# An adaLN block on one core: batch 1's normalised rows turned by VectorE and DMA, and a set of small edits to loads and scaling

## The reference

```python
mod = (_silu(c) @ wmod).reshape(4, 6, 1, 512)
sa, ca, ga, sb, cb, gb = (mod[:, i] for i in range(6))
ga = (2 * (ga >= 0) - 1) * jnp.maximum(jnp.abs(ga), 0.25)      # gb likewise
h = _layernorm(x) * (1 + ca) + sa
q, k, v = split(h @ Wqkv + bqkv)                                 # 128 columns each
attn = softmax(q @ k.T / sqrt(128)) @ v
x = x + ga * (attn @ Wo + bo)
h = _layernorm(x) * (1 + cb) + sb
top1 = argmax(h @ gate_w.T + expert_bias)                        # of 4 experts
x = x + gb * (h @ W_up.T + lora_B[top1] @ (lora_A[top1] @ h))
```

## Time and profile before

| | us |
|---|---|
| three timed runs | 182.58, 185.03, 185.26 (median 185.03) |
| profiled execution, whole | 182.96 |
| its span | 181.2 |
| TensorE busy in the span | 170.8 (94%) |
| VectorE busy | 139.6 (77%) |
| ScalarE, GpSimd busy | 90.1, 80.4 |

### The profile page before, as it was taken

One profiled execution on the slowest core, in us unless ns is written; L12 is line 12 of the kernel. 1 busy time (PEld: TensorE's weight loads), 2 busy tenths in 40 slices (PEclk: granted clock), 3 DMA queues, 4 the chain that ended last, 5 costly groups with the idle time before them and its releaser, 6 DMA issues.

```text
span 181.2 us, 2841 instructions
## 1 busy us (share of the span) xinstructions
PE 170.8 (94%) x924; PEld 134.9 (74%) x924; DVE 139.6 (77%) x352; ACT 90.1 (50%) x170; POOL 80.4 (44%) x109
## 2 busy tenths in 40 slices
PE   6867999999999999999999999999999999999990
...
GB/s 130 313 352 379 387 385 234 269 206 52 0 54 183 0 0 50 98 109 157 0 114 33 213 139 83 0 0 56 65 149 26 0 2 0 0 4 58 174 41 190
DMA packets 13918, 21.32 MB, mean 118 GB/s; under 512 B 3356, under 2 KB 4128, under 8 KB 13904
## 3 DMA queue, kind: packets, MB, share of 16 engines
...
## 4 chain that ended last, share of the span: by engine, by line
PE 57%; DVE 18%; ACT 8%; SPq 6%; DMA 6%; issue 4%; POOL 0%; DVEq 0%; ACTq 0%; POOLq 0%
PE bank L400 37%; SPq L322 5%; DMA stage<-in_L_wmod_dram 4%; PE bank L414 3%; DVE xs L1236 3%; ACT xn_p L849 3%; DVE stats L1243 3%; DVE xn L1169 2%; PE bank L524 2%; DVE f_gb L1301 1%; DVE h1lo L1158 1%; DVE h2lo L1174 1%; PE bank L509 1%; PE bank L503 1%; DMA stage<-xn 1%
## 5 line engine op out<-in xcount | busy, mean ns | idle before, releaser
L400 PE MATMUL bank<-wup_lo,h2hi 128*128 128x512 f32 (+1 forms) x68 | 27.2, 401 | 0.4 <-ACT h2hi L907 0.4
L400 PE MATMUL bank<-wup_hi,h2hi 128*128 128x512 f32 (+1 forms) x68 | 26.0, 382 | 0.0
L888 ACT ACTIVATE xn_p<-xs,shift,rstd 128x512 f32<-128x512 f32 x16 | 13.1, 816 | 25.9 <-POOL shift L1498 25.8
L400 PE MATMUL bank<-wup_hi,h2lo 128*128 128x512 f32 (+1 forms) x68 | 25.9, 381 | 0.0
L1495 POOL TENSOR_TENSOR rstd<-var_eps,neg_half 128x1 f32<-128x1 f32 x16 | 8.9, 554 | 37.2 <-DVE var_eps L1247 37.2
L1510 POOL TENSOR_TENSOR xs<-xs,f_gb 128x512 f32<-128x512 f32 x14 | 17.9, 1292 | 7.7 <-DVE f_gb L1301 7.7
L400 PE MATMUL bank<-h1lo,wqkv_hi 128*128 128x512 f32 x48 | 19.7, 411 | 1.6 <-ACT wqkv_hi L881 1.2
L1487 POOL TENSOR_TENSOR xs<-xs,gabo 128x512 f32<-128x512 f32 x16 | 20.3, 1308 | 0.1
L400 PE MATMUL bank<-h1hi,wqkv_hi 128*128 128x512 f32 x48 | 19.0, 395 | 0.0
L400 PE MATMUL bank<-h1hi,wqkv_lo 128*128 128x512 f32 x48 | 18.9, 394 | 0.0
L1219 DVE TENSOR_TENSOR plo<-bank,phi 128x512 fp32r<-128x512 f32 x16 | 10.0, 684 | 6.7 <-ACT phi L857 6.6
...
## 6 DMA issues: line engine op xcount, KB each, us to landing
...
stage<-in_L_wmod_dram SPq DMA_DIRECT2D x3, 1024.0 KB, 8.0
xs<-in_L_wmod_dram SPq DMA_DIRECT2D x3, 1024.0 KB, 7.6
xs<-in_L_attn_x_dram SPq DMA_DIRECT2D x3, 1024.0 KB, 8.4
...
f_gb<-in_L_ffn_W_up_dram SPq DMA_DIRECT2D x1, 1024.0 KB, 11.4
...
```

Source lines behind the costliest of these rows:

```text
L400: mm = nc.tensor.matmul(dst, w, m, start=first and i == 0, stop=last and i == total - 1)
L888: nc.scalar.activation(xn2_p[:, t, :], xs[:, b, t, :], ACT.Identity, bias=shift[:, 1, t:t + 1], scale=rstd[:, 1, t:t + 1]).then_inc(S["xn2 ...
```

## The change

- `TURNED` is 1: batch 1 too goes by blocks. Its 16 transposes on TensorE are gone; VectorE turns its four tiles around `qk_low(0)`, SyncE issues the 16 moves straight behind the load of gb, and x of batch 2 is loaded behind them. The first statistics of batch 2 stand behind batch 1's `h1_low`.
- Around that the order of the work changes: w_up's transposes come ahead of `pv(0)`, `modulation(3)` ahead of `out_projection(0)`, all of batch 1's qkv behind it.
- Loads: x of batch 0 in two halves, no waits between the first loads; sb and cb go to `f_gb`, w_up to `xs[:, 2]`; wo and bo ahead of w_up.
- ca is loaded and multiplied in two halves of 256 columns, each with its own bank.
- The scale of the scores is multiplied into Wq and q's bias by GpSimd (`scale_wq`), so `maxima` is one instruction per tile.
- eps of the second layer norm is added by GpSimd and not by VectorE.
- ga is spread over the partitions by transposes (line 445 before) and not by products.
- `gate_ffn(b - 1, 0)` stands ahead of the first tile's statistics.

The diff, cut to its core:

```diff
 
-TURNED = 2
...
+        (5, "cT"), (0, "x1T", 0, 0), (1, "x1T", 0, 1), (2, "x1T", 0, 2), (3, "x1T", 0, 3), (6, "mod", 0), (5, "ca_half"),
...
         (7, "PT", 0, 0), (1, "PT", 0, 1), (3, "PT", 0, 2), (0, "PT", 0, 3),
-        (2, "x1T", 1, 0), (4, "x1T", 1, 1), (6, "x1T", 1, 2), (7, "x1T", 1, 3), (5, "O", 0),
...
-        raw = {"ca": stage[:], "sa": xs[:, 2], "ga": xs[:, 3], "sb": stage[:], "cb": stage[:], "gb": xs[:, 3],
-               "wup": f_gb, "wqkv": xn2_p}
+        raw = {"ca": stage[:], "sa": xs[:, 2], "ga": xs[:, 3], "sb": f_gb[:], "cb": f_gb[:], "gb": xs[:, 3],
+               "wup": xs[:, 2], "wqkv": xn2_p}
...
             sp.dma_start(c_rows[0:B, :], c).then_inc(c_in, 16)
-            for i, ts in enumerate((slice(0, 1), slice(1, 2), slice(2, 4))):
-                sp.dma_start(xs[:, 0, ts], x_v[0, :, ts, :]).then_inc(x0_in[i], 16)
-            load_section("ca")
-            sp.wait_ge(x0_in[1], 16)
+            for i in range(2):
+                sp.dma_start(xs[:, 0, 2 * i:2 * i + 2], x_v[0, :, 2 * i:2 * i + 2, :]).then_inc(x0_in[i], 16)
+            for half in range(2):
+                sp.dma_start(raw["ca"][:, :, columns_of(half)], wmod_v[SECTION["ca"], :, :, columns_of(half)]).then_inc(ca_in[half], 16)
             load_wqkv((0, 1))
-            sp.wait_ge(x0_in[2], 16)
             load_section("sa")
             load_wqkv((2, 3))
             sp.wait_ge(S["bqkv_zero"], 1)
             sp.dma_start(bqkv_rows[0:B, :], bqkv.partition_broadcast(B)).then_inc(bqkv_in, 16)
             sp.dma_start(xs[:, 1], x_v[1]).then_inc(x_in[1], 16)
             load_section("ga")
-            wait_used(0)
             load_section("sb")
-            wait_used(1)
-            sp.dma_start(xs[:, 2], x_v[2]).then_inc(x_in[2], 16)
             sp.dma_start(wo_raw[:], wo).then_inc(wo_in, 16)
             sp.dma_start(bo_bc[:], bo.partition_broadcast(P)).then_inc(bo_in, 16)
-            sp.dma_start(raw["wup"][:], wup.rearrange("(o p) h -> p o h", p=P)).then_inc(wup_in, 16)
+            wait_used(1)
+            sp.dma_start(raw["wup"], wup.rearrange("(o p) h -> p o h", p=P)).then_inc(wup_in, 16)
             sp.dma_start(ga_rows[0:E, :], gate_w).then_inc(ga_rows_in, 16)
             sp.dma_start(ga_rows[E:GZ, :], lora_a.rearrange("e r h -> (e r) h")).then_inc(ga_rows_in, 16)
             for e in range(E):
...
             wait_used(2)
             load_section("cb")
             load_section("gb")
+            move_turned(1)
+            sp.wait_ge(S["wupT_psum"], NK)
+            sp.dma_start(xs[:, 2], x_v[2]).then_inc(x_in[2], 16)
             write_gate(0)
             spread_gate(0, 1)
             wait_used(3)
...
                     pe.wait_ge(mod_in[s], 16)
-                if g == 0:
-                    pe.wait_ge(S["silu_step"], 4)
                 quarters = [(s, kt) for s in GROUPS[g] for kt in range(0, NK, len(GROUPS[g]))]
                 for more in range(len(GROUPS[g])):
                     for i, (s, kt) in enumerate(quarters):
                         mm = nc.tensor.matmul(dst[i * QUARTER:(i + 1) * QUARTER, :], silu_wide[:, kt + more, :],
                                               raw[s][:, kt + more, :], start=more == 0, stop=more == len(GROUPS[g]) - 1)
                 mm.then_inc(S["mod_psum"], 1)
+
+            def first_modulation():
+
+                pe.wait_ge(S["silu_step"], 4)
+                for half in range(2):
+                    dst = open_bank("ca_half") if half else open_bank("mod", 0)
+                    pe.wait_ge(ca_in[half], 16)
+                    for kt in range(NK):
+                        mm = nc.tensor.matmul(dst[kt * QUARTER:(kt + 1) * QUARTER, columns_of(half)], silu_wide[:, kt, :],
+                                              raw["ca"][:, kt, columns_of(half)], start=True, stop=True)
+                    mm.then_inc(S["mod_psum"] if half else S["ca_half_psum"], 1)
 
             def first_modulation_columns(half):
...
@@ -719,16 +719,14 @@
             first_gate_everywhere()
             gate_to_rows("ga")
             p_transposes(0, (3,))
-            x1_transposes(1)
+            w_up_transposes(range(NK))
             pv(0)
-            w_up_transposes(range(NK))
-            qkv(1, (0,))
+            modulation(3)
             out_projection(0)
-            qkv(1, (1,))
-            modulation(3)
+            qkv(1, (0, 1))
             gate_transposes()
+            qkv(1, (2,))
             lora_b_transposes()
-            qkv(1, (2,))
             modulation_columns(3)
             qkv(1, (3,))
             x2_transposes(0)
...
                     nc.scalar.activation(xn2_p[:, t, :], at("S", b, t)[:], ACT.Exp, bias=neg_max[:, t:t + 1],
-                                         scale=SCORE_SCALE, accum_out=row_sum[:, t:t + 1]).then_inc(S["p_ready"], 1)
+                                         accum_out=row_sum[:, t:t + 1]).then_inc(S["p_ready"], 1)
...
@@ -878,6 +876,7 @@
 
             def wqkv_high(kt):
                 act.wait_ge(wqkv_in[kt], 16)
+                act.wait_ge(S["wq_scaled"], kt + 1)
...
             act.wait_ge(S["ga_bc_psum"], 1)
             nc.scalar.activation(ga_bc[:, 0, :], at("ga_bc")[:], ACT.Copy).then_inc(S["ga_bc_ready"], 1)
             pt_high(0, (3,))
-            h1_high(1, (0, 1))
+            wup_high((0, 1))
             wo_high(0)
-            h1_high(1, (2, 3))
+            wup_high((2, 3))
             o_high(0)
-            wup_high(range(NK))
+            h1_high(1)
+            modulation_rows(3)
             ln2_normalise(0, (0, 1))
-            modulation_rows(3)
...
                 dve.wait_ge(S["x1T_psum"], NK)
                 for t in range(NT):
-                    nc.vector.tensor_scalar(xn1[:, t, :], xs[:, 1, t, :], moments[:, 0, t, 0:1], rstd[:, 0, t:t + 1],
+                    nc.vector.tensor_scalar(xn1_blocks[:, :, :, t].rearrange("p a k i -> p k a i"),
+                                            xs[:, 1, t, :].rearrange("p (k a i) -> p k a i", k=NK, a=NB),
+                                            moments[:, 0, t, 0:1], rstd[:, 0, t:t + 1],
                                             ALU.subtract, ALU.mult).then_inc(S["xn1_ready"], 1)
...
-            def turn_blocks(b):
-                for t in range(NT):
+            def turn_blocks(b, tiles=range(NT)):
+                for t in tiles:
                     xn1_done(dve, b, t + 1)
                     nc.vector.transpose(xn1_blocks[:, :, :, t], xn1_blocks[:, :, :, t]).then_inc(S["xn1_turned"], 1)
...
             def maxima(b):
                 for t in range(NT):
                     dve.wait_ge(S["S_psum"], NT * b + t + 1)
-                    nc.vector.reduce_max(row_max[:, t:t + 1], at("S", b, t)[:], AX_X).then_inc(S["max_ready"], 1)
-                    dve.wait_ge(S["max_ready"], NT * b + t + 1)
-                    nc.vector.tensor_scalar(neg_max[:, t:t + 1], row_max[:, t:t + 1], -SCORE_SCALE, None,
-                                            ALU.mult).then_inc(S["negmax_ready"], 1)
+                    nc.vector.reduce_max(neg_max[:, t:t + 1], at("S", b, t)[:], AX_X, negate=True).then_inc(S["negmax_ready"], 1)
...
@@ -1243,9 +1241,6 @@
                 nc.vector.bn_stats(stats[:, 1, t, :], xs[:, b, t, :]).then_inc(S["ln2_stats"], 1)
                 dve.wait_ge(S["ln2_stats"], NT * b + t + 1)
                 nc.vector.bn_aggr(moments[:, 1, t, :], stats[:, 1, t, :]).then_inc(S["ln2_aggr"], 1)
-                dve.wait_ge(S["ln2_aggr"], NT * b + t + 1)
-                nc.vector.tensor_scalar(var_eps[:, 1, t:t + 1], moments[:, 1, t, 1:2], LN_EPS, None,
-                                        ALU.add).then_inc(S["ln2_var"], 1)
...
@@ -1343,9 +1338,11 @@
             widen_sa()
             second_ln1_normalise()
             qkv_shift_row()
+            turn_blocks(1, (0,))
             qkv_shift()
+            turn_blocks(1, (1, 2))
             qk_low(0)
-            ln1_stats(2, (0, 1))
+            turn_blocks(1, (3,))
             maxima(0)
             add_parts("ga")
             gate_columns("ga")
@@ -1353,17 +1350,19 @@
             v_low(0)
             pt_low(0)
             gate_rows_evacuate("ga")
-            h1_low(1)
+            wup_low(range(NK))
             split_sb()
             inverse_sums(0)
             o_low(0)
-            wup_low(range(NK))
+            h1_low(1)
+            ln1_stats(2, (0,))
             for t in range(NT):
                 residual(0, t)
...
+            ln1_stats(2, (1,))
...
                     for t in range(NT):
                         residual(b, t)
+                        if t == 0:
+                            gate_ffn(b - 1, 0)
                         ln2_moments(b, t)
-                        if t != 1:
-                            gate_ffn(b - 1, (0, 0, 1, 2)[t])
+                        if t >= 2:
+                            gate_ffn(b - 1, t - 1)
                     gate_ffn(b - 1, 3)
...
             def ln2_deviation(b, tiles):
```

(21 more changed lines are left out.)

43 lines of the change are left out of this document (18 added, 25 removed).

## The result

The changed kernel takes 185.22 us (median of 20 runs, 184.29 to 187.2), the kernel before 182.63 us beside it (181.89 to 186.07): a ratio of 1.016, interval 1.014 to 1.018. (The ratios of this text leave out executions in a slower state that the chip shows with either kernel, so this one differs a little from the ratio of the medians.) The change is slower by 1.6%, where I had forecast 181.7 us and a gain of 2.3; the time lies above my range, which ended at 184.8. The profiled execution took 185.26 us, its span is 183.5 (before 182.96 and 181.2).

The account below looks back on a forecast made before the run. TensorE bounds most of the span, but VectorE's new chain decides: 1.0 + 0.2 + 0.8 = 2.0 us by batch 2's scores, plus 0.3 at the end, gain 2.3. Middle of 180.7 and 182.8: 181.7 us, range 178.9 to 184.8.

Parts of the forecast that it names:

- TensorE's work: TensorE's queue: batch 1's 16 transposes go (1.75 us) and ga's products become transposes (0.56 us), together 2.3 us less.
- the scaling of Wq: On GpSimd between 11 and 17 us, four pieces: costed at nothing, under 1 us were the cover gone.
- A = 41.9: Landing of batch 1's last move: first move at 30.5 us, last begins 9.4 later and lands 2.02 after that.
- break-even of 42.9: VectorE ahead of batch 1's scores: landing time at which it breaks even; the forecast landing left it 1.0 us early.
- A + 3.6: VectorE after the last landing of batch 1's moves: its next own work after the four h1_lo begins 3.6 us later.
- The residual cycles (1.6 us): VectorE ahead of batch 1's scores: four residuals with their statistics, 1.6 us each instead of 1.81, 6.4 in all.
- From the second tile on a gain: Second normalisation, eps by GpSimd: 0.3 us each, a loss of 0.1 for a single tile, then a gain.
- 0.8 us of gain from four shorter residuals: Batch 2's chain up to its scores: four residuals 0.2 us shorter each, 0.8 of the 2.0 us gained there.
- The end: Last batch: earlier statistics close most of h2hi's 0.4 us wait, counted 0.3; f_gb's 0.4 wait goes too, not added.
- as I thought likeliest: Whole kernel: time within 2% (3.7 us) of before, the first and third cases, 0.68 less 0.03.
- My third: VectorE's chain eats the gain: landing at 44 by slower moves or late gb, gain 0.2, 182.8 us; chance 0.18.
- The fourth: SyncE can't issue the moves while cb and gb are on their way: landing at 49.4, 188.2 us; chance 0.10.

Follow-up runs that it names:

- e_no_turn: The changed kernel with batch 1's rows transposed by TensorE again, all other parts kept; 1.001 (0.998-1.004) against the kernel before.

## Why the turning costs: two engines at one port

Two of the turning's terms could be undone by order alone, so I tried these, the sum of them, and one of them without the turning.

```diff
 # f_quiet, against the changed kernel
-            add_output_bias(0)
+            add_output_bias(0, (0, 1))
+            pool.wait_ge(S["h1_lo"], NK * 2)
+            add_output_bias(0, (2, 3))
 # f_early_ga: batch 2's ga rows behind batch 1's, no longer behind the moves
             spread_gate(0, 1)
+            spread_gate(0, 2)
...
-                if b + 2 < B:
+                if b and b + 2 < B:
                     spread_gate(0, b + 2)
 # f_all: both, and eps on VectorE; f_best: e_no_turn with early rows and eps on VectorE
```

> The changed kernel; GpSimd adds the output bias to the first two tiles of batch 0 as it did, and waits with the last two until h1_lo of batch 1 is through. Theory (the first two h1_lo of batch 1 take 1361 and 1790 ns in place of 746 because GpSimd adds the bias to tiles 2 and 3 meanwhile, both engines reading two operands from SBUF): all four h1_lo take 0.75 us or less, VectorE's first residual starts 1.3 to 1.7 us earlier, tiles 2 and 3 of the bias (1.3 us each) are still in time for residuals 2 and 3, and the time falls by 1.0 to 1.6 us against the change: 0.7 to 1.1% above the kernel before. Rival (the long h1_lo come from the load of x2, which lands in xs at the same time): they stay at 1.4 to 1.8 us, the time stays at +1.6% or grows, since GpSimd is later.

> The changed kernel with batch 2's ga rows spread straight behind batch 1's, instead of behind the 16 moves of batch 2 and the two spreads of gb. Theory (at batch 1's second normalisation GpSimd is the chain, since ga's rows land only at 87.7 us and 2.6 us of output weights and bias stand ahead of the deviations): GpSimd does these between 83.3 and 86 us, where it waited 4.5 us; the last shift comes 1.8 to 3 us earlier, and the time falls by 1.5 to 2.5 us, to -0.2 ... +0.6% against before, though eps stays with GpSimd. Rival (VectorE's residuals and TensorE's queue set that end): 0.3 us or less, +1.4% or more.

> The changed kernel with all three undone costs: the bias of tiles 2 and 3 behind h1_lo, ga's rows for batch 2 spread early, eps on VectorE. Theory: the two places give 1.3 and 2.0 us, eps nothing more, since GpSimd is not the chain any longer (it may cost VectorE 0.2 us a tile); about 3 us below the change, -0.5 to 0.0% against before. Rival (the landing of the moves, 1.0 us behind my figure, and TensorE's own queue leave nothing more to win): no better than the single steps, +0.8%.

> The changed kernel without the turning of batch 1 (TensorE transposes it), with eps on VectorE and batch 2's ga rows spread early. Theory: without the turning the time was 0.1% above before, of which eps had about 0.5%; the early rows take GpSimd out of batch 1's second normalisation (idle 81.0 to 85.4 us there), worth 1 us more: -0.7 to -1.2% against before. Rival (eps and the early rows don't add up with the other parts): -0.4% or less of a gain. If this is faster than the kernel that has all three steps and the turning, the turning itself costs even where its two collisions are gone.

f_quiet gave 1.005, better than I expected. VectorE's timeline there:

```profile
44.09 2.74 DVE L1159 SCALAR_TENSOR_TENSOR h1lo<-stage,modT_ca,h1hi 128x512 fp32r<-128x512 f32 x4 [1.54 <-ACT h1hi L799]
47.46 0.70 DVE L1023 BATCH_NORM_STATS2 stats<-xs 128x6 f32<-128x512 f32 x1 [0.63 <-DMA xs<-in_L_attn_x_dram]
```

With GpSimd silent the four h1_lo take 2.74 us in place of 4.40, though the load of x2 is still under way (it lands only at 47.4). So the load is not the reason, and the 1.66 us are GpSimd's. This agrees with a rule of the Trainium skill that I had not applied: "SBUF — State Buffer", section "Who interferes with whom", says that a VectorE instruction with two inputs in SBUF contends with a GpSimd instruction that reads SBUF, and calls the pair of ports that they share an exclusive lock. The trace of the change agrees within 0.2 us: counted back from its end by the 0.75 us that it takes alone, the second h1_lo would begin at 46.02, where GpSimd's fourth addition ends at 46.23; and that addition, counted back by 1.30, at 44.93, where the first h1_lo ends at 45.06. That it is a port is the page's account; the traces show the durations.

The other three missed. f_early_ga gave 1.013, f_all 1.016, f_best 1.006, all far from what I expected. GpSimd and VectorE in f_early_ga:

```profile
82.86 1.30 POOL L1474 TENSOR_TENSOR wo_ga<-wo_raw,ga_bc 128x512 f32<-128x512 f32 x1
84.11 1.74 POOL L1479 TENSOR_TENSOR gabo<-bo_bc,ga_bc 128x512 f32<-128x512 f32 x1
```

```profile
83.09 4.64 DVE L1160 SCALAR_TENSOR_TENSOR h1lo<-stage,modT_ca,h1hi 128x512 fp32r<-128x512 f32 x4 [1.58 <-ACT h1hi L800]
```

The two products came 4.6 us earlier on the table's scale, as meant, and straight onto h1_lo of batch 2, which now took 4.64 us in place of 2.74; GpSimd's own product took 1.74 in place of 1.29. I had repaired one collision and built the same one somewhere else. f_all and f_best have it too (4.67 and 4.91 us). f_all shows how it adds up: it is 0.7 us ahead of the change at batch 2's moves and 1.3 at the last shift, in spite of the collision, but with eps on VectorE it is 82.5 us from qk_lo(2) to the end where the change is 81.6, and both end at 153.6.

## Both collisions gone

```diff
 # g_turn, g_best, g_before, g_moves_first: f_early_ga's early rows, and on GpSimd, batch 1
+                if not last:
+                    output_weights(b + 1)
+                    output_bias(b + 1)
                 if b == 1:
                     ln1_deviation(3)
                     ln1_offset(3)
-                if not last:
-                    output_weights(b + 1)
-                    output_bias(b + 1)
 # g_turn: on the change, with f_quiet's wait; g_best: on e_no_turn; g_before: on the kernel before
 # g_moves_first: g_turn, and
-            wait_used(2)
-            load_section("cb")
-            load_section("gb")
             move_turned(1)
             sp.wait_ge(S["wupT_psum"], NK)
             sp.dma_start(xs[:, 2], x_v[2]).then_inc(x_in[2], 16)
+            wait_used(2)
+            load_section("cb")
+            load_section("gb")
...
-            modulation(3)
             out_projection(0)
...
+            modulation(3)
             modulation_columns(3)
```

> The changed kernel with GpSimd kept off VectorE's h1_lo at both places: the bias of batch 0's last two tiles behind h1_lo of batch 1; batch 2's ga rows spread early and their two products (output weights, bias) done straight after batch 1's bias, ahead of the third normalisation's deviations, so that they end before h1_lo of batch 2 begins. Eps stays with GpSimd. Theory (early rows gained nothing by themselves because the two products then ran beside h1_lo of batch 2, whose four took 4.64 us in place of 2.74): h1_lo of batch 2 takes 2.75 us, the last shift of batch 1 comes 2 to 4 us earlier than the change's 98.17, and the time falls to between -0.9 and -0.2% against before. Rival (the end of batch 1's second normalisation is set by something else, TensorE's queue or VectorE's residuals): +0.5% as with the first wait alone.

> The same ordering of ga's rows and of GpSimd's two products, in the changed kernel without the turning of batch 1. Theory: without the collision and with GpSimd out of the way the last shift of batch 1 comes some 3 us earlier than in the kernel without turning (95.82), TensorE's 1.9 us wait for the second normalisation goes, and the time is 0.7 to 1.3% below before. If it is faster than the kernel with turning, turning batch 1 costs by itself; if it is slower, the turning's gain on TensorE (1.75 us) was there and was hidden by the collisions. I expect the two within 0.4% of each other.

> The kernel before with nothing but the early ga rows and GpSimd's two products ahead of the third deviations. Theory: GpSimd's chain through batch 1's second normalisation (85.86 to 94.46 us) ends 1 to 2 us earlier; TensorE waits only 0.8 us there (f_gb, h2hi), so the time falls by 0.3 to 0.8 us: -0.2 to -0.5%. Rival (that chain bounds nothing in the kernel before): 0.0%.

> The kernel of the first run of this set (turning kept, GpSimd off both places), and the 16 moves of batch 1 and the load of x2 stand ahead of the loads of cb and gb; the fourth modulation moves behind batch 1's projections. Theory (the last move lands 3.0 to 3.3 us after its issue begins, against 2.0 for batch 2, because 2 MB of cb and gb are in the queues before it, and it begins 0.9 us later because of their issue): the last landing comes 1.5 to 2 us earlier relative to the first maximum of batch 0, x2 lands before h1_lo ends, and TensorE's wait ahead of batch 1's scores shrinks by 1 us or more; time 0.3 to 0.8% below the first run of this set. Rival (cb and gb are then late and the fourth modulation, or the shift rows behind it, stall TensorE): same or slower.

g_turn gave 0.998 and g_best 0.990, the fastest kernel of this study: 181.16 us against 182.92. GpSimd in g_best:

```profile
72.12 1.29 POOL L1477 TENSOR_TENSOR wo_ga<-wo_raw,ga_bc 128x512 f32<-128x512 f32 x1
73.36 1.28 POOL L1482 TENSOR_TENSOR gabo<-bo_bc,ga_bc 128x512 f32<-128x512 f32 x1
...
85.86 0.23 POOL L1498 TENSOR_SCALAR var_eps<-moments 128x1 f32<-128x1 f32 x1 [4.15 <-DVE moments L1251]
```

The products lie where neither VectorE's h1_lo nor a deviation wants GpSimd, and the first deviation waits for VectorE, not the other way round. The last still waits for GpSimd: VectorE has its moments at 91.14, and GpSimd comes to its eps at 92.64, behind a product of f_gb. g_before shows no clear gain (0.998, interval over 1): its last shift did not move (64.43 and 64.42). In the kernel before VectorE has the last tile's variance ready at 93.38 and GpSimd is free for it at 93.58, so the two chains end together there, and freeing one is worth little. I had expected -0.2 to -0.5%; the interval does not exclude it.

The turning still costs 0.8% by the timed runs (0.998 against 0.990; by the two traces 0.8 us, 0.4%). g_moves_first missed as well, at 1.013. Its moves landed much as theory had it: a median of 2.0 us each against 5.1 in g_turn, the last after 2.5, and the last landing 1.5 us earlier on the table's scale. So most of what the change's last move takes over 2.0 us comes from the 2 MB of cb and gb ahead of the moves. But the rival was right on what follows: without the fourth modulation between them, TensorE waits 1.6 us for o_lo ahead of the output products, and the late modulation holds what stands behind it; qk_lo(1) is through only at 32.73.

## What the turning costs by itself

```diff
 # h_half_moves, against g_turn; the count that is waited for is 8 moves lower. It leaves out half
 # of the moves, so batch 1 is computed from wrong rows: a probe of its time alone
-            move_turned(1)
+            move_turned(1, (0, 1))
 # h_pool_moves, against g_turn
-            move_turned(1)
+            move_turned(1, (0, 1, 2))        # and the last four by nc.gpsimd.dma_start
 # h_tensor_eps: g_best with eps on VectorE
```

> The kernel with the turning and with GpSimd kept off both places, and only 8 of batch 1's 16 moves are issued; half of batch 1's turned rows are thus not those of batch 1 and its result is not the reference's. Nothing else is left out. Theory (the length of the chain of moves is what the turning costs by itself): the last landing, h1_hi and the load of x2 come 5 us earlier, VectorE is no longer late ahead of batch 1's scores, TensorE's 1.75 us of transposes become a gain, and the time is 1.5 to 2.2% below before, clearly below the version that turns batch 1 on TensorE (-1.0%). Rival (the price lies in VectorE's longer list, not in the landing: the turns, query lows by tokens at 1.8 in place of 1.4 us, residuals): within 0.3% of the kernel with 16 moves, -0.5 to 0.0%.

> The kernel with the turning and with GpSimd kept off both places, and the last 4 of batch 1's 16 moves are issued by GpSimd, idle between 30.0 and 36.0 us. Theory (the issue of the moves, 0.63 us each one behind the other on SyncE, sets the last landing): SyncE is through 2.5 us earlier, x2 is asked for near 37.7 us (behind TensorE's w_up transposes) in place of 41.3, and the time falls by 0.5 to 1.2% against the kernel with all moves on SyncE, to -0.7 ... -1.4% against before. Rival (the backlog of cb and gb in the queues sets the landing, not the issue): the last landing stays at 42 us or later and the time within 0.3%. Third case: GpSimd takes over 1 us for each issue and its output weights come late: slower.

> The fastest version so far (batch 1 turned by TensorE, early ga rows, GpSimd's products before the third deviations), with eps added by VectorE again. Theory (eps by GpSimd cost time only because GpSimd was the chain at batch 1's second normalisation): now that it is not, VectorE's 0.2 us a tile come back onto the chain of residuals and the time rises by 0.3 to 0.8 us: -0.8 to -0.5% against before. Rival (eps by GpSimd costs 0.3 us a tile wherever it stands): -1.2% or faster.

h_half_moves gave 0.990. That is 0.8% better than g_turn, so the length of the moves' chain, with what stands behind it on SyncE's queue, carries the turning's cost; the rival (VectorE's list) had 1.000 to 0.995. But it isn't the 1.5 to 2.2% that the theory had, and not a bit better than g_best, which leaves the 1.75 us of transposes on TensorE. Its VectorE shows what comes next:

```profile
41.50 0.69 DVE L1227 TENSOR_TENSOR o_lo<-bank,o_hi 128x512 fp32r<-128x512 f32 x1 [0.54 <-ACT o_hi L864]
42.12 3.71 DVE L1160 SCALAR_TENSOR_TENSOR h1lo<-stage,modT_ca,h1hi 128x512 fp32r<-128x512 f32 x4
45.74 0.68 DVE L1024 BATCH_NORM_STATS2 stats<-xs 128x6 f32<-128x512 f32 x1
46.35 0.73 DVE L1235 SCALAR_TENSOR_TENSOR xs<-bank,row_inv,xs 128x512 f32<-128x512 f32 x1
```

VectorE has no gap left there: h1_lo follows o_lo at once (and meets GpSimd's bias of tiles 0 and 1, 3.71 us), and still its first residual starts at 46.35, where g_best's starts at 45.12 (16.4 against 15.5 on the table's scale), and TensorE waits 0.8 us in all for qk_lo. But that is not shown to be VectorE's list: the collision that came back takes 0.97 of it (3.71 against 2.74 us). What the turning would be worth with early moves and no collision was not run.

h_pool_moves gave 0.997, as g_turn. GpSimd issued its four in 2.25 us, SyncE was through at 38.97 and not 41.25, and yet the last moves landed later (median 6.7 us from issue, up to 9.1; h1_lo started at 14.6 us after the first maximum, against 13.7): gb itself landed 9.5 us after the first maximum, against 7.5. So the landing follows the data on their way and not the issue, as the rival had it.

h_tensor_eps gave 0.993 against g_best's 0.990; the intervals overlap. Its last shift is even 0.8 us earlier than g_best's, but the time from qk_lo(2) to the end is 82.4 in place of 81.7. The earlier shift is what the last tile's wait for GpSimd in g_best would lead one to expect, so the premise that GpSimd was out of the chain held for the first deviation only. The two effects nearly cancel; the sign of what is left is not settled.

## Why the prediction was wrong, step by step

- **TensorE's work.** The transposes went, but its busy time fell only from 170.8 to 169.9 us, not by 2.3. No record is missing: there are 924 and 912 matmuls, 16 and 4 fewer and 8 more for ca in halves. The halves add 0.2 us that I had not counted (2 x 0.64 for 1.07). The rest I put down to the new standstills: products start 0.23 us apart but are recorded as 0.40 long, so that each one ahead of a standstill counts 0.17 more (an estimate). TensorE starts at 14.8 us (15.1 foretold), and nothing of it reaches the scores, as I had counted. But the scaling of Wq, costed at nothing, takes 538 ns a piece on GpSimd, ScalarE waits for it, and the last h1_lo of batch 0 is through at 18.68 and not 18.01. Batch 1's rows had landed at 17.73, yet VectorE's statistics of them begin only at 18.59, and at 25.23 TensorE gives its lead up in a wait of 0.57 us for the bias row (`qb_row`): the scaling cost what the head had won.
- **A = 41.9, the last landing.** Measured 42.86. The issue began at 30.03 (30.5 foretold) and its last started 9.54 us later (9.4), but the landing took 3.29 in place of 2.02. I took the landing of batch 2's moves, made on idle queues; here cb and gb were ahead. 1.0 us, and with it the whole margin to my break-even of 42.9.
- **"A + 3.6" to the end of h1_lo.** This is the step that failed. It was read off batch 2's moves, where GpSimd waits for ga's rows; for batch 1 it is 5.2 (48.10), by the collision with the output bias, 1.66 us. I had named VectorE's queue and its waits, but had not asked what the other engines do to its instructions' durations. The residual cycles (1.6 us) were right, qk_lo's 1.67 as well (1.69). The sum foretold 58.0 for qk_lo's end; measured 60.88, 2.9 later, of which 1.0 is the landing and 1.7 the collision. Nor had I asked whether TensorE would wait for batch 0's second normalisation, which hangs on the same residuals: it did, 1.8 us, twice as long as for qk_lo.
- **"From the second tile on a gain" for eps by GpSimd.** Wrong in the sign at batch 1. I had priced it against VectorE's chain, though the earlier trace rows of before ran there with GpSimd in series behind ga's late rows. The step costs 1.5 us at batch 2's scores and gives 0.8 back later. So where I had 0.8 us of gain from four shorter residuals there was a loss.
- **The end.** The waits for f_gb and h2hi closed as foretold, and TensorE got 1.0 us back behind batch 2's scores. +3.3 at qk_lo(2) less 1.0 is the +2.3 us of the span.
- **The cases.** My third (VectorE's chain eats the gain, 182.8) had the right mechanism, with a price from moves alone and no second bottleneck. The fourth (SyncE can't issue) did not come: the moves were issued at 0.64 us each. The time stayed within 2% of the kernel before, as I thought likeliest, but on the other side of it and so not for my reason, and above my range, as no case had a loss between 0 and 5 us. (A slip of 0.1 us in the numbers decides nothing: 185.03 - 2.3 is 182.7.)
